# Moving an expert's output bias from VectorE's read of the result into TensorE's accumulation

## The chip, the cores and the metric

The kernel runs on one core of a Trainium2 chip. The metric is device time in microseconds (us), and lower is better. Three runs of the kernel before took 2040.01, 2044.2 and 2039.57 us, with a median of 2040.01 us.

## The reference

The reference is four layers on 4096 tokens of width 128 (16 sequences of 256 tokens). The change touches only layer 0, whose attention part is a selective state scan (256 inner channels, 16 states) and whose feed-forward part is a mixture of 16 experts, of which 12 have weights. For each of those twelve:

```
h = gelu(x_e @ w1[e] + b1[e])      # x_e: up to 512 tokens x 128, h: 512 x 512
y = h @ w2[e] + b2[e]              # 512 x 128
```

The rows y are written to a buffer in memory, from which each token later gathers the two rows that it is owed and adds them with their weights. Everything is float32.

## The kernel before, in words

In `mamba_scan` the state scan and the twelve experts of layer 0 run in one interleaved program. The scan is cut in 128 steps q: one step handles two states of one sequence for both halves of the channels, so it holds two units i = 2q and 2q + 1. For every unit

- ScalarE writes the decays exp(delta * a) in a PSUM bank (L874, two instructions),
- GpSimd multiplies the input with the spread-out B rows (L740),
- VectorE runs the scan (L952) and multiplies its result with the spread-out C rows (L958),
- TensorE adds the product over the states in the bank Y (L785).

Once a step, TensorE spreads C (`spread_c`, L770) and B (`spread_b`, L761) over the partitions, and ScalarE copies B to SBUF (L884). VectorE's product L958 waits for `c_ready`, which the last L770 of its step raises; ScalarE's copy L884 waits for `b_ready`, which L761 raises. Once a sequence there are also the gate product (L965), the skip term (L778), the output projection (L798, L799) and its copy (L888).

Each engine's order is written out by hand. TensorE's order in a step is: `spread_c(q)`, `sum_states(2q-1)`, `spread_b(q+2)`, `expert(q, 0)`, at the first step of a sequence the skip term, `sum_states(2q)`, at one step the projection, `expert(q, 1)`. There is no reordering, so what stands in `expert` stands ahead of the next `spread_c`.

An expert takes a new place every 6 steps. Its work: transpose of its tokens (L836), copy (L896), first product (L828, four matmuls 128x512 in two steps), gelu by ScalarE (L905, four), second product (L811), VectorE's read of the result with the bias (L971) and the store. The second product fills four blocks of 128 tokens of bank 7 (`E1_BANK`), one block in each `expert(q, part)` call of two successive steps; a block is four float32 matmuls 128x128 that accumulate over the hidden width. The first block waits for the last gelu of the expert (`act_done`). The last block raises `y_ready`, and VectorE reads the bank after the first unit of the next step.

The expert's weights lie packed in `ew`; columns B2 to B2 + 128 hold the bias b2, the same row in all 128 partitions. `g.ident` is the 128x128 float32 identity.

Of the kernel before, what the change touches and what calls it, by code (L numbers as in the profile page):

```python
# [9 lines left out]
ALU = mybir.AluOpType  # L10
# [3 lines left out]
P = 128  # L14
D = 128
# [24 lines left out]
FC = F0 // P  # L40
# [38 lines left out]
def rows(ap):  # L79
    return ap.rearrange("p a b -> p (a b)")  # L80
# [515 lines left out]
def mamba_scan(nc, g, t, u, gate_d, delta, bc3, sel, disp, ybuf, r, scattered, f):  # L596
# [4 lines left out]
    DA, C_BANK, E0_BANK, BO, Y_BANK, E1_BANK = 0, 3, 4, 5, 6, 7  # L601
    RING = 3
    NE, CT = E0 - FIRST_MLP0, CAP0 // P
    W2, B1, B2, WN = FC * P, 2 * FC * P, 2 * FC * P + FC, 2 * FC * P + FC + D
# [8 lines left out]
    with section(nc, "scan", *names, "skip_made", "skip_used", "zeroed", "du_ready", "b_ready", "b_copied", "bu_made",  # L613
# [10 lines left out]
        ew = s.sb("ew", [P, 2, WN])  # L624
        exin = s.sb("exin", [P, 2, CT, D])
        ext = s.sb("ext", [P, CAP0])
        eht = s.sb("eht", [P, FC, CAP0])
        eyo = s.sb("eyo", [P, CT, D])
# [7 lines left out]
        def bank(i):  # L636
            return g.ps[:, i, :].rearrange("p (n t) -> p n t", t=T)

        def row(i):
            return sel[:, i:i + 1].to_broadcast([3 * 2 * DS, P])  # L640

        def phase(q, offset):
            e, rest = divmod(q - FIRST - offset, SPACING)
            return e if rest == 0 and 0 <= e < NE else None
# [11 lines left out]
        with nc.Block() as block:  # L656
# [93 lines left out]
            @block.tensor  # L750
            def _(pe):
                def spread_b(q):
                    if q >= NQ:
                        return
                    b, pr = divmod(q, PAIRS)
                    if q >= 1:
                        pe.wait_ge(s.b_copied, q)
                    if b >= 1 and pr == 4:
                        pe.wait_ge(s.o_taken, b)
                    for n in range(2):  # L760
                        ins = nc.tensor.matmul(bank(BO)[:, n, :], row(2 * pr + n), bc3[:, b * T:(b + 1) * T],  # L761
                                               start=True, stop=True)
                    ins.then_inc(s.b_ready, 1)

                def spread_c(q):
                    b, pr = divmod(q, PAIRS)
                    if q >= 1:
                        pe.wait_ge(s.hc_ready, 2 * q)
                    for n in range(2):
                        ins = nc.tensor.matmul(bank(C_BANK)[:, n, :], row(DS + 2 * pr + n),  # L770
                                               bc3[:, b * T:(b + 1) * T], start=True, stop=True)
                    ins.then_inc(s.c_ready, 1)

                def skip_term(b):
                    if b >= 1:
                        pe.wait_ge(s.yg_ready, b)
                    pe.wait_ge(s.skip_made, b + 1)
                    nc.tensor.matmul(g.ps[:, Y_BANK, :], g.ident[:], rows(skip[:]), start=True,  # L778
                                     stop=False).then_inc(s.skip_used, 1)

                def sum_states(i):
                    q, c = divmod(i, DC)
                    pe.wait_ge(s.hc_ready, i + 1)
                    for n in range(2):
                        ins = nc.tensor.matmul(bank(Y_BANK)[:, c, :], g.ident[:], hc[:, i % RING, n, :], start=False,  # L785
                                               stop=(i % (PAIRS * DC) == PAIRS * DC - 1 and n == 1))
                    ins.then_inc(s.sum_done, 1)

                def project(b, ahead):
                    pe.wait_ge(s.yg_ready, b + 1)  # L790
                    if ahead < NQ:
                        pe.wait_ge(s.b_copied, ahead)
                    else:
                        pe.wait_ge(s.combined, 2 * NGRP)
                    for k in range(QT):
                        out = g.ps[:, BO, k * D:(k + 1) * D]
                        for c in range(DC):
                            nc.tensor.matmul(out, yg[:, c, k * P:(k + 1) * P], w_out[:, c, :], start=(c == 0), stop=False)  # L798
                        ins = nc.tensor.matmul(out, g.ident[:], g.x[:, b * QT + k, :], start=False, stop=True)  # L799
                    ins.then_inc(s.o_ready, 1)  # L800

                def expert(q, part):
                    for half, offset in ((0, DOWN0), (1, DOWN1)):
                        e = phase(q, offset)
                        if e is None:
                            continue
                        pe.wait_ge(s.act_done, (e + 1) * FC)
                        i = 2 * half + part
                        out = g.ps[:, E1_BANK, i * D:(i + 1) * D]
                        for f in range(FC):  # L810
                            ins = nc.tensor.matmul(out, eht[:, f, i * P:(i + 1) * P],  # L811
                                                   ew[:, e % 2, W2 + f * P:W2 + (f + 1) * P], start=(f == 0),
                                                   stop=(f == FC - 1))
                        if i == CT - 1:
                            ins.then_inc(s.y_ready, 1)
                    for half, offset in ((0, UP0), (1, UP1)):
                        e = phase(q, offset)
                        if e is None:
                            continue
                        if half == 0 and part == 0:  # L820
                            pe.wait_ge(ew_in[e % 2], (e // 2 + 1) * 16)
                            pe.wait_ge(s.xt_ready, e + 1)
                        if half == 0 and part == 1 and e >= 1:
                            pe.wait_ge(s.y_out, e)
                        if half == 1:
                            pe.wait_ge(s.act_done, e * FC + part + 1)
                        f = 2 * half + part
                        nc.tensor.matmul(g.ps[:, (E0_BANK, E1_BANK)[part], :], ew[:, e % 2, f * P:(f + 1) * P], ext[:],  # L828
                                         start=True, stop=True).then_inc(s.h_ready, 1)
                    e = phase(q, TURN)  # L830
                    if e is not None and part == 1:
                        pe.wait_ge(ex_in[e % 2], (e // 2 + 1) * 16)
                        if e >= 1:
                            pe.wait_ge(s.act_done, e * FC)
                        for i in range(CT):
                            ins = nc.tensor.transpose(g.ps[:, E0_BANK, i * P:(i + 1) * P], exin[:, e % 2, i, :],  # L836
                                                      g.ident[:])
                        ins.then_inc(s.turned, 1)

                spread_b(0)  # L840
                spread_b(1)
                for q in range(NQ):
                    b, pr = divmod(q, PAIRS)
                    spread_c(q)
                    if q >= 1:
                        sum_states(2 * q - 1)
                    if b >= 1 and pr == 3:
                        spread_b(q + 1)
                    elif not (b >= 1 and pr == 2):
                        spread_b(q + 2)  # L850
                    expert(q, 0)
                    if pr == 0:
                        skip_term(b)
                    sum_states(2 * q)
                    if b >= 1 and pr == 2:
                        project(b - 1, q + 2)
                    if b >= 1 and pr == 3:
                        spread_b(q + 2)
                    expert(q, 1)
                sum_states(NU - 1)  # L860
                project(BATCH - 1, NQ)
# [81 lines left out]
            def _(dve):  # L943
                v = nc.vector
# [22 lines left out]
                def take_result(e):  # L967
                    dve.wait_ge(s.y_ready, e + 1)
                    if e >= 1:
                        dve.wait_ge(s.stored, e * 16)  # L970
                    v.tensor_tensor(eyo[:], g.ps[:, E1_BANK, :].rearrange("p (t d) -> p t d", d=D),  # L971
                                    ew[:, e % 2, None, B2:B2 + D].to_broadcast([P, CT, D]), ALU.add).then_inc(s.y_out, 1)

                def combine(j, k):
                    dve.wait_ge(weighted[k], j + 1)
# [7 lines left out]
                for q in range(NQ):  # L983
# [4 lines left out]
                    e = phase(q, DOWN1 + 1)  # L988
# [2002 lines left out]
```

## Time and profile before

| | before |
|---|---|
| median of 3 runs | 2040.01 us (2039.57 to 2044.2) |
| profiled execution: time | 2040.01 us |
| profiled execution: span, first to last instruction | 2038.2 us |
| mean granted TensorE clock (1 is 2.4 GHz) | 0.883 |
| TensorE matmul busy | 1564.5 us (77%) |
| VectorE busy | 1293.2 us (63%) |
| ScalarE busy | 1057.1 us (52%) |
| GpSimd busy | 797.3 us (39%) |
| scan with experts | about 220 to 585 us of the span |
| scan with gather | about 585 to 820 us |

The profiled execution has the median's time, 1.8 us more than its span. In the rows PE is TensorE's matmul, PEld its weight load, DVE VectorE, ACT ScalarE and POOL GpSimd; busy matmuls overlap, since their ends are modelled, so starts are the better measure. A float32 matmul is two records, each with a weight load and a matmul: L811 has 384 records for 12 x 4 x 4 = 192 matmuls. In matmul records the operands are listed as output<-moving,stationary. A row of the timeline gives start, duration, engine, line, operation, count, and in brackets the idle time before it with what ended it.

### The profile page before, as it was taken

Reading aid. Unit: us, or ns where it says so; the run is one execution under the profiler, and the core shown is the slowest. Engines: PE = TensorE matmul, PEld = TensorE weight load, DVE = VectorE, ACT = ScalarE, POOL = GpSimd, SP = SyncE. Lnnn points to the kernel's source line nnn. Section 1 sums busy time; section 2 is a strip of 40 time slices with the busy share of each in tenths; the row PEclk is TensorE's granted clock in tenths of the full one; section 3 lists DMA queues with packets and bytes.
Section 4 is the critical chain, followed back from the end, with each engine's and each line's share of the span. In section 5 each row is a group of like instructions: output and inputs, shape, how many; then the busy total and the mean of one; then the engine's idle time right before and its main releaser. Section 6 shows DMA issues by size and latency. Waiting matters only on the chain. (4 is left out here: it accounts for less than half of the span.)

```text
span 2038.2 us, 34107 instructions
## 1 busy us (share of the span) xinstructions
PE 1564.5 (77%) x12145; PEld 1073.5 (53%) x12146; DVE 1293.2 (63%) x2310; ACT 1057.1 (52%) x1921; POOL 797.3 (39%) x803
## 2 busy tenths in 40 slices
PE   6918688888877667641999999984699999749975
PEld 5605366665654444510667776652245444537853
DVE  7403888787788888751644457858763897624324
ACT  1204888887876666240544455554464777314421
POOL 1570566565679997275012233331500000050041
PEclk9959799999998898675899999997699999669987
DMA  5201111111000010571421125512641341211311
GB/s 153 81 30 37 50 54 50 40 48 45 28 27 26 26 32 11 215 214 39 66 58 58 58 57 84 83 26 81 127 86 52 47 66 19 90 52 39 109 41 55
DMA packets 153335, 130.56 MB, mean 64 GB/s; under 512 B 18929, under 2 KB 137864, under 8 KB 152914
## 3 DMA queue, kind: packets, MB, share of 16 engines
q1 hardware_dynamic: 140554, 104.54, 20.9%
q0 software_dynamic: 12544, 23.82, 4.3%
q8 instruction: 100, 1.64, 0.4%
q14 instruction: 65, 0.53, 0.1%
q10 hardware_dynamic: 72, 0.03, 0.0%
HBM read 77.08 MB, written 52.43 MB: 64 GB/s over the span
## 5 line engine op out<-in xcount | busy, mean ns | idle before, releaser
L740 POOL TENSOR_TENSOR xn_t<-xn_t,scan_du 128x512 f32<-128x512 f32 x256 | 321.2, 1273 | 144.4 <-ACT xn_t L884 97.4
L952 DVE TENSOR_TENSOR_SCAN xn_t<-banks,xn_t 128x512 f32<-128x512 f32 x256 | 311.8, 1218 | 73.3 <-ACT banks L874 44.9
L785 PE MATMUL banks<-scan_hc,ident 128*128 128x256 f32 x1024 | 294.9, 414 | 51.1 <-DVE scan_hc L958 51.1
L2383 ACT ACTIVATE att_pr<-banks 128x768 f32<-128x768 f32 (+1 forms) x256 | 234.4, 917 | 126.1 <-PE banks L2275 75.6
L874 ACT ACTIVATE banks<-delta,scan_exp_centre,a_neg 128x255 f32<-128x255 f32 x512 | 266.1, 561 | 15.7 <-DVE xn_t L952 15.1
L785 PEld LDWEIGHTS banks<-scan_hc,ident 128*128 128x128 f32 x1024 | 192.7, 206 | 111.7 <-DVE scan_hc L958 73.6
L958 DVE TENSOR_TENSOR scan_hc<-xn_t,banks 128x512 f32<-128x512 f32 x256 | 175.9, 687 | 25.8 <-PE banks L770 10.9
L2427 DVE TENSOR_REDUCE att_mb<-banks 128x6 f32<-128x768 f32 x128 | 121.8, 956 | 103.3 <-remote 51.6
L2242 PE MATMUL banks<-att_ks,att_qs 48*128 48x256 bf16 (+1 forms) x1024 | 111.8, 275 | 80.1 <-DVE att_mb L2427 30.4
L1009 POOL DMA_INDIRECT disp<-xn_tok,places x128 | 135.6, 1059 | 73.3 <-issue 38.4
L2431 DVE TENSOR_REDUCE att_mb<-banks 128x4 f32<-128x1024 f32 x128 | 153.8, 1222 | 15.9 <-PE banks L2242 10.6
L2291 PE MATMUL banks<-att_pr,att_vx 128*32 128x256 f32 (+1 forms) x2048 | 154.6, 374 | 8.7 <-ACT att_ot L2388 6.8
L884 ACT COPY xn_t<-banks 128x512 f32<-128x512 f32 x128 | 74.8, 584 | 108.3 <-PE banks L761 86.8
L1394 POOL DMA_DIRECT2D ybuf<-att_yo x72 | 39.0, 542 | 207.8 <-DVE att_yo L1379 204.2
L1210 POOL IOTA gau_rev<- 128x8 f32 x1 | 0.1, 138 | 298.8 <-POOLq L76 298.8
L2267 PE MATMUL banks<-att_qs,att_ks 50*128 50x256 bf16 (+1 forms) x1024 | 108.1, 268 | 8.5 <-DMA att_qs<-att_mt 6.7
L2242 PEld LDWEIGHTS banks<-att_ks,att_qs 48*128 48x128 bf16 x1024 | 48.2, 98 | 102.2 <-issue 39.4
L1295 PE MATMUL banks<-grouped_w,att_xt 128*128 x288 | 99.5, 469 | 0.6 <-DVE att_xt L1361 0.4
L1584 POOL DMA_INDIRECT gau_gb<-ybuf,rows x32 | 32.4, 1014 | 146.0 <-DMA ybuf<-gau_eyo 136.6
L1344 ACT ACTIVATE att_a<-banks 128x352 f32<-128x352 f32 x72 | 33.4, 464 | 99.4 <-PE banks L1295 99.4
L770 PE MATMUL banks<-bc,state_sel 96*128 96x256 bf16 x256 | 53.0, 291 | 34.6 <-DVE scan_hc L958 32.4
L449 PE MATMUL banks<-xn_t,w_taps 128*128 128x255 f32 (+2 forms) x256 | 64.0, 399 | 19.4 <-issue 18.2
(384 smaller groups left out, 3290.4 us busy)
## 6 DMA issues: line engine op xcount, KB each, us to landing
scan_ew<-f_packed SPq DMA_DIRECT2D x12, 578.0 KB, 4.1
q_parts<-att_p_parts SPq DMA_DIRECT2D x16, 384.0 KB, 4.2
k_parts<-att_p_parts SPq DMA_DIRECT2D x16, 384.0 KB, 6.1
att_qs<-q_parts SPq DMA_DIRECT2D x64, 96.0 KB
att_ks<-k_parts SPq DMA_DIRECT2D x64, 96.0 KB
gau_ew<-f_packed SPq DMA_DIRECT2D x8, 578.0 KB
disp<-zeros SPq DMA_DIRECT2D x1, 4608.0 KB, 15.4
att_xin<-disp SPq DMA_DIRECT2D x72, 64.0 KB
```

Source lines behind the costliest of these rows:

```text
L740: nc.gpsimd.tensor_tensor(bu[:, i % RING], b_sb[:, q % 2], du[:, b % 2, c:c + 1, :].to_broadcast([P, 2, T]), ALU.mult).then_inc(s.bu_made, 1)
L785: ins = nc.tensor.matmul(bank(Y_BANK)[:, c, :], g.ident[:], hc[:, i % RING, n, :], start=False, stop=(i % (PAIRS * DC) == PAIRS * DC - 1 a ...
L874: ins = nc.scalar.activation(bank(DA + i % RING)[:, n, 1:T], delta[:, c, b * T + 1:(b + 1) * T], ACT.Exp, scale=a_neg[:, c, state:state + ...
L952: v.tensor_tensor_scan(rows(h[:, i % 2]), g.ps[:, DA + i % RING, :], rows(bu[:, i % RING]), 0.0, ALU.mult, ALU.add).then_inc(s.scan_done, 1)
L958: v.tensor_tensor(hc[:, i % RING], h[:, i % 2], bank(C_BANK), ALU.mult).then_inc(s.hc_ready, 1)
L1009: pool.indirect_dma_start(disp, bass.IndirectOffsetOnAxis(ap=r.scat_i[:, k, i:i + 1], axis=0), src[:, i, :], None, bounds_check=disp.shape ...
L2242: ins = nc.tensor.matmul(g.ps[:, 2 * m_slot(i) + half, lo:hi], qs[rows_of, p, j, q * P:(q + 1) * P], ks[rows_of, p, j, 0:hi - lo], start=T ...
L2267: ins = nc.tensor.matmul(g.ps[:, 2 * s_slot(i) + half, k * T:k * T + T - q0], ks[rows_of, p, j, k * P:(k + 1) * P], qs[rows_of, p, j, q0:T ...
L2291: ins = nc.tensor.matmul(g.ps[r * 32:(r + 1) * 32, O_BANK, q0:T], vx[:, b % 2, k, 4 * jg + r, :], pr[:, i % RING, half, k * T:k * T + T - q0],
L2383: nc.scalar.activation(pr[:, i % RING], g.ps[:, at:at + 2, 0:W], ACT.Exp, scale=scale).then_inc(s.p_ready, 1)
L2427: v.tensor_reduce(mb[:, b % 2, j, :].rearrange("p (g n) -> p g n", g=2), g.ps[:, at:at + 2, 0:W].rearrange("p g (n k) -> p g n k", k=P), A ...
L2431: v.tensor_reduce(mb[:, b % 2, j, :], g.ps[:, at:at + 2, :].rearrange("p g (n k) -> p (g n) k", k=T), AX_X, ALU.max).then_inc(s.m_taken, 1)
```

## The change

Each block of the second product gets a fifth matmul. Its stationary operand is column 0 of the identity, broadcast to 128 columns, so its first row is ones and the others zeros, and its moving operand is the bias row: it adds b2 to each of the 128 tokens. It is the last of the accumulation and takes over `stop` and, in the last block, the increment of `y_ready`. VectorE's read of the bank becomes a plain copy.

```diff
@@ expert(q, part), TensorE @@
                         for f in range(FC):
-                            ins = nc.tensor.matmul(out, eht[:, f, i * P:(i + 1) * P],
-                                                   ew[:, e % 2, W2 + f * P:W2 + (f + 1) * P], start=(f == 0),
-                                                   stop=(f == FC - 1))
+                            nc.tensor.matmul(out, eht[:, f, i * P:(i + 1) * P],
+                                             ew[:, e % 2, W2 + f * P:W2 + (f + 1) * P], start=(f == 0), stop=False)
+                        ins = nc.tensor.matmul(out, g.ident[:, 0:1].to_broadcast([P, P]), ew[:, e % 2, B2:B2 + D],
+                                               start=False, stop=True)
                         if i == CT - 1:
                             ins.then_inc(s.y_ready, 1)
@@ take_result(e), VectorE @@
-                    v.tensor_tensor(eyo[:], g.ps[:, E1_BANK, :].rearrange("p (t d) -> p t d", d=D),
-                                    ew[:, e % 2, None, B2:B2 + D].to_broadcast([P, CT, D]), ALU.add).then_inc(s.y_out, 1)
+                    v.tensor_copy(rows(eyo[:]), g.ps[:, E1_BANK, :]).then_inc(s.y_out, 1)
```

## Rows read from the trace of the kernel before

**Rows 1.** Windows: each engine's busy time (instructions), granted clock, DMA share and GB/s.
```profile
220.00:585.00 365.00, 305.40 (x1586) 225.34 (x1586) 297.13 (x331) 299.10 (x511) 228.77 (x190) 0.96 0.15 45
820.00:2038.00 1218.00, 965.06 (x9387) 642.83 (x9385) 702.44 (x1514) 548.47 (x990) 290.05 (x349) 0.87 0.32 76
```

**Rows 2.** Waits, 220 to 580 us: us in total, times, longest.
```profile
ACT xn_t L884 <- PE banks L761: 47.8, 37, 3.0
PE banks L811 <- ACT scan_eht L905: 18.9, 12, 3.3
DVE scan_hc L958 <- PE banks L770: 10.9, 8, 2.0
```

**Rows 3.** Timeline of one expert's second product, from its first matmul to VectorE's read.
```profile
282.89 1.16 PE L811 MATMUL banks<-scan_ew,scan_eht 128*128 128x128 f32 x8 [1.19 <-ACT scan_eht L905]
283.88 1.03 PE L785 MATMUL banks<-scan_hc,ident 128*128 128x256 f32 x4
...
284.75 1.05 PE L811 MATMUL banks<-scan_ew,scan_eht 128*128 128x128 f32 x8
...
285.64 0.60 PE L836 MATMUL banks<-ident,scan_exin 128*128 128x128 f32 x4
...
286.08 0.38 PE L770 MATMUL banks<-bc,state_sel 96*128 96x256 bf16 x2
...
286.55 0.69 DVE L958 TENSOR_TENSOR scan_hc<-xn_t,banks 128x512 f32<-128x512 f32 x1
...
287.38 1.05 PE L811 MATMUL banks<-scan_ew,scan_eht 128*128 128x128 f32 x8
...
289.14 1.05 PE L811 MATMUL banks<-scan_ew,scan_eht 128*128 128x128 f32 x8
...
290.03 0.38 PE L770 MATMUL banks<-bc,state_sel 96*128 96x256 bf16 x2
...
290.51 0.69 DVE L958 TENSOR_TENSOR scan_hc<-xn_t,banks 128x512 f32<-128x512 f32 x1 [0.28 <-DVE xn_t L952]
...
291.11 0.68 DVE L971 TENSOR_TENSOR scan_eyo<-banks,scan_ew 128x512 f32<-128x512 f32 x1
291.12 0.38 PE L761 MATMUL banks<-bc,state_sel 96*128 96x256 bf16 x2
...
291.54 0.59 ACT L884 COPY xn_t<-banks 128x512 f32<-128x512 f32 x1 [0.93 <-PE banks L761]
291.71 1.22 DVE L952 TENSOR_TENSOR_SCAN xn_t<-banks,xn_t 128x512 f32<-128x512 f32 x1
```

**Rows 4.** Windows of TensorE alone, two experts: busy (records), clock, DMA.
```profile
282.89:290.40 7.51, 7.51 (x55) 1.00 0.12 35
394.92:404.04 9.12, 9.12 (x55) 0.82 0.10 30
```

**Rows 5.** Timeline, VectorE's product before its read, in other experts.
```profile
261.94 0.69 DVE L958 TENSOR_TENSOR scan_hc<-xn_t,banks 128x512 f32<-128x512 f32 x1 [0.33 <-DVE xn_t L952]
345.53 0.69 DVE L958 TENSOR_TENSOR scan_hc<-xn_t,banks 128x512 f32<-128x512 f32 x1 [1.40 <-issue]
576.57 0.69 DVE L958 TENSOR_TENSOR scan_hc<-xn_t,banks 128x512 f32<-128x512 f32 x1 [1.02 <-issue]
```

**Rows 6.** One line's instructions, L2554: duration min/median/max in ns, starts.
```profile
L2554 PEld LDWEIGHTS banks<-norm_mix,mixes_lora_bi x2: 192/192/192, 853.7 to 853.8; 128*128 128x128 f32 x2
L2554 PE MATMUL banks<-norm_mix,mixes_lora_bi x2: 275/275/275, 853.8 to 853.9; 128*128 128x128 f32 x2
```

**Rows 7.** Groups of instructions by shape, VectorE: busy us, mean ns, idle before.
```profile
L971 DVE TENSOR_TENSOR scan_eyo<-banks,scan_ew 128x512 f32<-128x512 f32 x12 | 8.2, 684 | 0.0
L539 DVE COPY front_dtx<-banks 128x512 f32<-128x512 f32 x8 | 5.5, 689 | 28.2 <-PE banks L422 21.1 <-remote 7.0
```

**Rows 8.** Timeline of TensorE, the expert whose second product begins at 394.92 us.
```profile
394.92 2.08 PE L811 MATMUL banks<-scan_ew,scan_eht 128*128 128x128 f32 x8 [1.19 <-ACT scan_eht L905]
...
396.78 1.75 PE L785 MATMUL banks<-scan_hc,ident 128*128 128x256 f32 x4
```

## The prediction

> **What bounds the kernel now.** I read the windows first, to see how full the engines are where the change lies. In the stage that holds scan and experts no engine is full: of 365 us TensorE's matmuls fill 305.4, VectorE 297.1, ScalarE 299.1 [rows 1]. Some 60 us of TensorE's time look free, and on the average alone one would say that 48 short matmuls vanish in them. So the average can't settle it, and I went to the waits of the stage. Three of them tell how the engines hang together: TensorE waits twelve times for ScalarE's gelu before the second product, once an expert (18.9 us); ScalarE waits for the spread B rows of TensorE (37 times, 47.8 us); VectorE's product waits for the spread C rows (10.9 us) [rows 2]. The stage is a ring of four engines that wait for one another in a fixed order, and the question is who is last in the very place where the matmuls are added.
>
> The timeline of one expert answers that. Its second product begins at 282.89, when the gelu is done. From there the reader is to follow TensorE's starts: two blocks of L811 (282.89 and 284.75) with sums and a transpose between them, L770 at 286.08, two more blocks (287.38 and 289.14), L770 at 290.03 [rows 3]. TensorE's window over this stretch is 7.51 us long and busy for 7.51 us [rows 4]: not a gap. At its end L770 starts at 290.03 and takes 0.38, so it ends at 290.41, and VectorE's product starts at 290.51, after 0.28 us of idling [rows 3]. The row names the scan L952 as releaser, but VectorE's own scan is simply the instruction before it; what came 0.10 us before the start is the end of L770, the same distance as between 286.46 and 286.55 one step earlier. ScalarE idles for 0.93 us and starts its copy at 291.54, just after L761 (291.12 + 0.38 = 291.50) [rows 3]. So at the end of an expert's second product VectorE and ScalarE both stand and wait for TensorE, and GpSimd's product needs ScalarE's copy and VectorE's scan. TensorE sets the pace of this stretch from the gelu on, although it doesn't set that of the stage.
>
> I looked at the same place in all twelve experts. VectorE idles ahead of the product that precedes its read in every one: 0.28 us in six of them, 0.33 in three, 1.40 in two and 1.02 in the last [rows 3, 5]. Where "issue" is named, L770 again ended just before. The case of the longer waits is the one where the output projection also stands in TensorE's queue.
>
> **The change part by part.** *Added on TensorE*: a fifth matmul in each block, 12 experts x 4 blocks = 48. Its shape is that of the four before it, 128x128 in float32. Its duration in the rows (about 275 ns a record) isn't what it costs, since matmuls overlap; the distance between starts is. From 284.75 to 285.64, the next instruction's start, four matmuls took 0.89 us, or 0.223 us each (two records of 0.11) [rows 3]. The one thing that is new is the stationary operand, one column repeated. L2554 loads such an operand in float32: its two records start 0.1 us apart and take 192 and 275 ns [rows 6], which is what ordinary ones take, so I take no surcharge. The bounds: below, a single record of 0.11, were the load hidden; above, what a matmul costs at the low clock. That last price is in the trace too: the block at 394.92 took until 396.78, or 0.465 us a matmul [rows 8], at 1.2 GHz (granted 0.82 over the whole stretch, against 1.00 in the other) [rows 4].
>
> The added matmuls of a block stand behind the block and ahead of everything else in TensorE's queue: the sums L785, the skip term, the transpose, the projection, and both spreads. Behind the first two of an expert L770 at 286.08 comes 0.45 us later, and the product at 286.55 starts 0.09 us after its end now: it can't take up a delay of 0.45. Behind all four L770 at 290.03 comes 0.89 later, and the product at 290.51 with it, and L761 and ScalarE's copy too. Every engine had its wait in this stretch already, so none has slack left that would be used up later on; the whole ring moves by 4 x 0.223 = 0.89 us an expert. What comes next, the two L828 of the next expert and its gelu, waits for the same instructions, so it moves as well.
>
> The sum: 48 x 0.223 = 10.7 us. In four of twelve experts (second products from 394.92, 424.60, 511.23 and 540.79; [rows 8] is the first of them) a block or two run at the low clock, so I take 5 of 48 added matmuls at 0.465: + 5 x 0.24 = 1.2 us.
>
> *Removed on VectorE*: the addition of the bias; a copy of the same 128x512 out of PSUM takes its place. L971 takes 684 ns; a float32 copy of 128x512 from PSUM, L539, takes 689 [rows 7]. So that saves nothing: 12 x 0.005 = 0.06 us, if anything as a loss. It would matter if it did save: the read stands between the product and the next scan (290.51, 291.11, 291.71) on the engine that waited. The bounds are nothing and, by the widest guess, a copy in half of L539's time: 12 x 0.34 = 4.1 us. I take nothing, as the copy's row has the same engine, shape, type and memories. The Trainium skill ("VectorE: DVE Perf Modes", "Mode 2×_2P — use both read ports for one tensor") says that a copy in float32 goes twice as fast only with source and target both in SBUF, and that PSUM has one read port; the row of L539 agrees. By its fast mode the sum would be 4.1 us lower, by its rule for PSUM it stays.
>
> *Moved*: `y_ready` is raised by the fifth matmul of the last block, 0.22 us later than before in its block. VectorE asks for it only after the product that waits for L770, which comes still later in TensorE's queue, so this wait is never last. No DMA is added or moved in its queue; SP's store and weight loads wait for the read and shift with it. Nothing in the stages behind the experts changes.
>
> Total: 10.7 + 1.2 + 0.06 = 11.9 us on the profiled execution's 2040.01 us, which is also the median: **2051.9 us**, 0.6% slower.
>
> **The rivals.** *Part of it is hidden.* If the delay of each expert's first two matmuls were taken up, because VectorE's own chain is as late there (it idles only at the second L770, not at the first [rows 3]), only 24 matmuls count: 24 x 0.223 = 5.4, so 2045.4 us. Against it: TensorE is busy without a gap from 282.89 on [rows 4], so what is added at the start is still there at the end. Chance 0.06.
>
> *All is hidden*: the 60 us of TensorE's idle time in the stage [rows 1] take it up. Then 2040.0 us. For that the idle time would have to lie inside the stretch of the second product; it lies before it, in the wait for the gelu [rows 2, 3]. Chance 0.03.
>
> *The clock gives it back, and more.* This is the case that ends faster. After its wait for the gelu TensorE ran at the low clock in the stretch at 394.92, and its 7.51 us became 9.12 [rows 4]. If the added matmuls, by making TensorE busier, kept the clock at 2.4 GHz, each such stretch would get back 1.61 us, four of them 6.4 us, and the result would be 2040.0 + 11.9 - 6.4 = 2045.5. To be faster by 0.3% it must get back 11.9 + 6.1 = 18 us. The stage can't: its clock of 0.96 over 365 us [rows 1] means 2 x 0.04 x 365 = 29 us at half speed, which hold 15 us to gain at most if every one were on the path. It would need the stages behind 820 us, with 0.87 [rows 1], where the kernel is unchanged and only shifted in time. The point from which it decides is thus 36 us of low clock turned to high, half of it on the path. Chance 0.06 for the clock to give back a good part, of which 0.03 for faster. The Trainium skill ("TensorE: Matmul & The Clock Gate", "What's actually happening") says that activity lifts the throttle and idleness sets it; that more matmuls lift it here no row can show.
>
> *Short matmuls are cheaper than the rows' distance.* If a record beside others cost half of what stands between starts now, 0.056 us, the sum would be 48 x 0.11 = 5.3 us and the time 2045.3. The rows speak against it: eight records behind one another take 0.89 us at full clock [rows 3]. Chance 0.02. The Trainium skill ("TensorE: Matmul & The Clock Gate", "Back-to-back issue gap") has a gap of about 56 ns for 128 columns of bf16, the distance of this rival; the trace has 0.11 for a float32 record.
>
> **How the numbers follow.** My forecast, the delay in full, has chance 0.83. Its own range is 10.7 us with no low clock at all to 10.7 + 48 x 0.24 x 0.25 = 13.6 with a quarter of them at low clock, and 1.5 us either side for where the low clock falls in the later stages (the three runs of before spread over 4.6 us): 2049 to 2055. The partly hidden case, the short matmuls and the clock at 2045.4 are taken in as well: the whole range is 2045 to 2055.5. About 0.3%, or 6.1 us, is what a measurement of this kernel tells from no change. Slower by more (over 2046.1): 0.83. Within: 0.06 + 0.03 + 0.03 + 0.02 = 0.14. Faster: 0.03.
>
> **What the profile of the changed kernel would show.** TensorE's records at the second product grow by 96, starts 0.11 us apart. From the gelu to the second L770's end an expert at full clock takes 7.51 + 0.89 = 8.4 us, still without a gap. VectorE's idle time before the product that precedes its read grows by about 0.45 us (0.28 to about 0.7), since the other 0.45 is met at the first L770; there an idle time of about 0.4 appears that is not there now. L971 keeps its 0.68 to 0.69 us. The stage from the first scan to the last expert's read is 11 to 12 us longer, the stages behind it as long as before. I would be wrong if an expert's period of 6 steps grew by less than 0.8 us though its TensorE stretch grew by 0.89 (then there is slack that I missed), if the new load took longer than an ordinary one, or if the clock's low stretches moved by more than a few us.

## The result and the profile after

The changed kernel took 2054.34 us in the median of nine runs (2047.3 to 2057.14), the kernel before 2043.53 us in nine (2039.57 to 2048.34). The ratio is 1.0053, with a 95% interval of 1.0038 to 1.0068: slower by about 11 us, between 8 and 14. The prediction, 2051.9 us with slower at 0.83, holds, and its sum of 11.9 us lies inside that interval. The absolute time came out 2.4 us over it although the difference came out 1.1 us under, since the kernel before itself took 3.5 us more in nine runs than in the three that the prediction started from. The profiled execution took 2063.16 us with a span of 2061.4 us, which is 8.8 us above the median of its runs, so this one profile is read by its stretches and not by its whole span.

The timeline of the changed kernel at the place of [rows 3]; L813 is the added matmul, and the lines behind it are numbered one higher than before:

```profile
281.95 1.16 PE L811 MATMUL banks<-scan_ew,scan_eht 128*128 128x128 f32 x8 [1.12 <-ACT scan_eht L906]
...
282.94 0.39 PE L813 MATMUL banks<-scan_ew,ident 128*128 128x128 f32 x2
283.17 1.03 PE L785 MATMUL banks<-scan_hc,ident 128*128 128x256 f32 x4
...
285.58 0.38 PE L770 MATMUL banks<-bc,state_sel 96*128 96x256 bf16 x2
...
286.06 0.69 DVE L959 TENSOR_TENSOR scan_hc<-xn_t,banks 128x512 f32<-128x512 f32 x1 [0.54 <-PE banks L770]
...
289.76 0.39 PE L813 MATMUL banks<-scan_ew,ident 128*128 128x128 f32 x2
289.99 0.38 PE L770 MATMUL banks<-bc,state_sel 96*128 96x256 bf16 x2
...
290.46 0.69 DVE L959 TENSOR_TENSOR scan_hc<-xn_t,banks 128x512 f32<-128x512 f32 x1 [0.73 <-DVE xn_t L953]
291.07 0.68 DVE L972 COPY scan_eyo<-banks 128x512 f32<-128x512 f32 x1
...
291.49 0.59 ACT L885 COPY xn_t<-banks 128x512 f32<-128x512 f32 x1 [1.40 <-PE banks L761]
```

The added matmul stands from 282.94 to 283.17, 0.23 us. At the first L770 VectorE now idles 0.54 us where its row showed nothing (0.45 us of delay and the 0.09 us that were there); at the second it idles 0.73 us in place of 0.28, and ScalarE 1.40 in place of 0.93. TensorE's stretch, in the windows of the changed kernel (columns as in [rows 1]):

```profile
281.95:290.36 8.41, 8.41 (x63) 7.94 (x64) 5.88 (x7) 7.76 (x14) 4.70 (x5) 1.00 0.10 31
```

Against 7.51 us and 55 records [rows 4] that is 0.90 us and 8 records more, without a gap. The whole stage from the first to the last scan takes 605.0 us (scans start from 221.1 to 826.1) against 592.0 (223.7 to 815.7): 13.0 us more, and all of it lies ahead of the last expert's read (366.4 us from the first scan against 353.4). What lies behind the last scan took 1235.3 us against 1222.5, though nothing is changed there. In the first eight experiments below that part took between 1210 and 1225 us, on either side of before, and 1223.8 with the same added matmuls (e2); I take the 12.8 us for scatter of the single execution.

### The profile page after: what moved, and what is told of

It is laid out like the page before. It is cut to its first block and busy times, and to the rows that moved or that the text cites. A ratio compares the mean times of both kernels' runs of the same rounds, so it can differ in the third digit from the quotient of the medians.

```text
span 2061.4 us, 34299 instructions
## 1 busy us (share of the span) xinstructions
PE 1583.8 (77%) x12241; PEld 1089.1 (53%) x12242; DVE 1293.2 (63%) x2310; ACT 1056.0 (51%) x1921; POOL 796.1 (39%) x803
## 5 line engine op out<-in xcount | busy, mean ns | idle before, releaser
L770 PE MATMUL banks<-bc,state_sel 96*128 96x256 bf16 x256 | 53.3, 292 | 35.2 <-DVE scan_hc L959 32.4
L2267 PEld LDWEIGHTS banks<-att_qs,att_ks 50*128 50x128 bf16 x1024 | 39.9, 95 | 71.7 <-issue 41.4
```

What stands on the lines that cost most here:

```text
L2267: ins = nc.tensor.matmul(g.ps[:, 2 * s_slot(i) + half, k * T:k * T + T - q0], ks[rows_of, p, j, k * P:(k + 1) * P], qs[rows_of, p, j, q0:T ...
```

## The experiments

Ratios are to the kernel before on the same chip, with 95% intervals. Because the whole kernel's runs scatter by some us, I also read from each profile one stretch in which nothing but the scan and the experts runs: from the start of the second expert's second product to the start of the twelfth's, ten experts' periods. It holds ten experts' work, so the change's 48 matmuls count there with 40.

| kernel | ratio (interval) | stretch of ten periods, us | granted clock in it |
|---|---|---|---|
| before | 1 | 285.37 | 0.97 |
| the change | 1.0053 (1.0038 to 1.0068) | 295.78 | 0.96 |
| e1_copy_only | 0.9999 (0.998 to 1.0018) | 285.17 | 0.96 |
| e2_matmul_only | 1.0057 (1.0035 to 1.0079) | 295.92 | 0.96 |
| e3_two_more | 1.0105 (1.0082 to 1.0129) | 304.69 | 0.97 |
| e4_first_half | 1.0001 (0.9979 to 1.0023) | 286.93 | 0.98 |
| e5_last_half | 0.9995 (0.9978 to 1.0013) | 288.75 | 0.97 |
| e6_bf16 | 1.0005 (0.9986 to 1.0024) | 286.18 | 0.98 |
| e7_in_gelu_wait | 0.9965 (0.9946 to 0.9984) | 283.03 | 0.98 |
| e9_act_read_pool_add | 0.9999 (0.9984 to 1.0014) | 289.02 | 0.95 |
| e10_filled_waits | 0.9948 (0.993 to 0.9965) | 277.85 | 1.00 |
| e11_change_filled | 1.0003 (0.9987 to 1.0018) | 286.83 | 1.00 |
| e12_before_again | 1.0009 (0.9993 to 1.0026) | 288.84 | 0.95 |
| e13_gelu_wait_again | 0.9965 (0.9949 to 0.9981) | 280.56 | 0.99 |

The last four ran on a chip on which the kernel before took 1864.04 us (median of 35), since the parts around the scan were shorter there; their ratios are to that.

**The two halves of the change.** First VectorE's half alone:

```diff
-                    v.tensor_tensor(eyo[:], g.ps[:, E1_BANK, :].rearrange("p (t d) -> p t d", d=D),
-                                    ew[:, e % 2, None, B2:B2 + D].to_broadcast([P, CT, D]), ALU.add).then_inc(s.y_out, 1)
+                    v.tensor_copy(rows(eyo[:]), g.ps[:, E1_BANK, :]).then_inc(s.y_out, 1)
```

> VectorE's read is the plain copy, as in the changed kernel, and TensorE has no added matmul; the addition of b2 is left out. My theory: the copy costs what the addition did (L539 took 689 ns, L971 684), so the time stays within 1 us of before and the read stays at 0.68 us. Rival, the copy is the gain that the matmuls buy: at half of 0.68 us it would save 12 x 0.34 = 4.1 us, and the changed kernel's loss would hide that gain.

Measured 2041.27 us against 2042.64. The line of its read in the profile (duration min/median/max in ns, first and last start in us), to set beside [rows 7]:

```profile
L971 DVE COPY scan_eyo<-banks x12: 683/684/686, 260.1 to 574.5; 128x512 f32<-128x512 f32 x12
```

The copy takes the addition's 684 ns to the ns, and the kernel its time. The interval alone, 4 us either way, would just leave room for the rival's 4.1; the row and the stretch of ten periods (285.17 us against 285.37) rule it out. Then TensorE's half alone:

```diff
@@ expert(q, part), in before; the four matmuls of the loop have stop=False @@
+                        ins = nc.tensor.matmul(out, g.ident[:, 0:1].to_broadcast([P, P]), ew[:, e % 2, B2:B2 + D],
+                                               start=False, stop=True)
```

> The 48 added matmuls alone; VectorE keeps its addition, so b2 is added twice. My theory: the whole change in time is TensorE's, so this takes as long as the changed kernel, 11 to 13 us over before (+10.8 us was measured for the change, and the stage from the first scan to the last was 13.0 us longer in its profile). Rival, the two halves of the change balance: this is slower than the changed kernel by as much as the copy saves, 4 us.

Measured 2052.09 us, by the ratio 11.6 us more (7 to 16); its stage from first to last scan is 605.2 us (the change: 605.0) and its stretch 295.92 us (295.78). So the loss is TensorE's alone, and no gain of VectorE's stands behind it.

**More of the same.**

```diff
@@ the changed kernel @@
+                        nc.tensor.matmul(out, g.ident[:, 0:1].to_broadcast([P, P]), ew[:, e % 2, B2:B2 + D],
+                                         start=False, stop=False)
                         ins = nc.tensor.matmul(out, g.ident[:, 0:1].to_broadcast([P, P]), ew[:, e % 2, B2:B2 + D],
                                                start=False, stop=True)
```

> The changed kernel with a sixth matmul in each block, equal to the fifth, so b2 is added twice. My theory: there is no slack anywhere in the second product, so each matmul counts 0.223 us at full clock; 96 of them cost 21.4 us plus 2 to 3 us for those at the low clock, twice the change's own. Expected over before: 22 to 25 us. Rival, the first added matmuls pay for a fixed delay (a longer accumulation, the new kind of stationary operand), and the next are cheaper: under 18 us. Rival, the clock stays up with more work: under 18 us too, with a mean clock over the scan stage nearer to 1.

Measured 2061.51 us against 2042.64, by the ratio 21.4 us more (17 to 26), just under the 22 to 25 that I expected; the stage is 615.8 us, 23.8 over before. The expert that begins at 283.77 runs at full clock:

```profile
283.77:293.07 9.30, 9.30 (x71) 8.83 (x72) 5.80 (x7) 7.77 (x14) 5.58 (x5) 1.00 0.09 28
```

7.51, 8.41 and 9.30 us with none, four and eight added matmuls: each costs 0.22 us, the first as much as the second. So the rival of a fixed delay falls. The rival of a clock that stays up falls by the stage and by the granted clock of 0.97 in the ten periods, the same as in before; the runs' interval, which reaches down to 17 us, would not exclude it by itself.

**Where the matmul stands.** Half of them each, ahead of the first or of the second spread of C (`half` is 0 or 1) in e4 and e5, with VectorE's addition kept:

```diff
@@ expert(q, part), in before; in these blocks the four matmuls of the loop have stop=False @@
+                        if half == 0:        # e4; half == 1 in e5
+                            ins = nc.tensor.matmul(out, g.ident[:, 0:1].to_broadcast([P, P]),
+                                                   ew[:, e % 2, B2:B2 + D], start=False, stop=True)
```

> Before with the added matmul in the first two blocks of each expert only (24 in all), and VectorE's addition kept. My theory: nothing of the delay at the first spread of C is taken up, although VectorE does not idle there before; so half of the full cost, 24 x 0.223 = 5.4 us, and 1 to 2 us more, since it is the first blocks that meet the low clock: 5.4 to 7.5 us over before. Rival, VectorE's chain is as late there and hides it: 0 to 2 us.

> Before with the added matmul in the last two blocks of each expert only (24), and VectorE's addition kept. VectorE idles at least 0.28 us in the product ahead of its read, so these matmuls are on the path without question: 24 x 0.223 = 5.4 us over before, hardly any of it at the low clock: 5 to 6 us. The two halves add up to the whole, 11 to 13 us, if the delay passes on in full everywhere; if the first half is hidden, this one alone makes up the whole.

Both came out within noise of before, where I had expected 5.4 us and more; 5.4 us lies outside both intervals (at most +4.7 and +2.7 us). Yet in both profiles the stretch from the first L811 to the second L770 of an expert, 7.14 us at full clock in before (282.89 to 290.03), was 7.59 and 7.60 us in the second expert: 0.45 us more, as reckoned, for the first half as for the second. It is not made up later in the expert either: an expert's period that ran wholly at full clock took 28.09 or 28.69 us in before, by its place in the sequence, and 28.53 or 28.54 and 29.13 in both of these, 0.44 to 0.45 us more. The stage from the first to the last scan was 594.5 us with the first half and 597.8 with the second, 2.5 and 5.8 over the 592.0 of before. So the profiles hold the delay, and the medians of the twelve runs do not show it. That is a miss of my expectations, and its cause stays open; what the clock can have to do with it is said below.

**Cheaper matmuls.**

```diff
+        none_b = s.sb("none_b", [P, D], BF16)
...
+                nc.gpsimd.memset(none_b[:], 0.0)
...
@@ expert(q, part), in before; the four matmuls of the loop have stop=False @@
+                        ins = nc.tensor.matmul(out, g.ident_b[:, 0:1].to_broadcast([P, P]), none_b[:],
+                                               start=False, stop=True)
```

> Before with a fifth matmul in each block whose operands are bf16, a column of the identity repeated and a tile of zeros; VectorE keeps its addition. My theory: the cost is TensorE's time in the place, whatever it adds. bf16 matmuls of 256 columns (L770 to L785, 0.22 us for two) go 0.11 us apart, so one of 128 columns takes 0.06 to 0.11 us; 48 x that is 2.7 to 5.3 us over before. Rival, a fifth matmul costs by being one more instruction with one more weight load, not by its passes: 10 us or more as in float32.

The same stretch of the second expert took 7.48 us (282.11 to 289.59), 0.34 more than before's 7.14, or 0.085 us a matmul, and the time did not change measurably (48 x 0.085 = 4.1 us is inside the interval, the rival's 10 us are not). The delay goes with the time that the added matmul takes TensorE, not with the number of instructions: a bf16 matmul of this shape is one record and 0.085 us, a float32 one two records and 0.223 us.

**In a wait.**

```diff
@@ expert(q, part), in before @@
+                        if half == 0 and part == 0:
+                            pe.wait_ge(s.act_done, (e + 1) * FC - 1)
+                            for _ in range(2):
+                                nc.tensor.matmul(g.ps[:, E0_BANK, 0:D], g.ident[:, 0:1].to_broadcast([P, P]),
+                                                 ew[:, e % 2, B2:B2 + D], start=True, stop=True)
                         pe.wait_ge(s.act_done, (e + 1) * FC)
```

> Before, with two matmuls of the same kind an expert put into TensorE's wait for the last gelu: they start when the third gelu is done and write the bank that it read, and their result is thrown away. 24 added matmuls, 24 x 0.223 = 5.4 us of work. My theory: what matters is where they stand, and here the last gelu (0.68 us) still runs, so 0.45 us is hidden and the time stays within 1 us of before. Rival, any work on TensorE in this stage costs its time (through the clock, or the queue): 5 to 6 us over before.

Not only was nothing lost: the kernel was faster, 2036.42 us against 2042.64. Its timeline at one expert, where L810 are the added ones:

```profile
365.76 1.26 ACT L910 ACTIVATE scan_eht<-banks,scan_ew 128x512 f32<-128x512 f32 x2
...
366.50 0.71 PE L810 MATMUL banks<-scan_ew,ident 128*128 128x128 f32 x4 [0.60 <-ACT scan_eht L910]
...
367.08 1.16 PE L816 MATMUL banks<-scan_ew,scan_eht 128*128 128x128 f32 x8
```

They begin after the third gelu. The last of their four records starts at 366.93, ahead of the fourth gelu's end at 367.02, and the second product starts at 367.08, 0.06 us behind that end, the same distance as in before (282.83 and 282.89). The expert's period that ends with this wait, at full clock, is 28.69 us with them (338.39 to 367.08) as without (336.79 to 365.48). The same instruction that costs its whole time behind the block costs nothing here. Where the gain of 7.1 us (by the ratio) comes from, this profile says only in part: its stage is 590.3 us, 1.7 under before, with a granted clock of 0.98 in the ten periods against 0.97.

**VectorE's read.** The prediction had said that the read lies on the path. If so, ScalarE and GpSimd could do it in their waits. ScalarE's copy comes one step later than VectorE's read did:

```diff
@@ scalar: new, called behind decay(2 * q) at phase(q, DOWN1 + 2); gone from vector @@
+                    act.wait_ge(s.y_ready, e + 1)
...
+                    nc.scalar.copy(rows(eyo[:]), g.ps[:, E1_BANK, :]).then_inc(s.y_out, 1)
@@ gpsimd: behind the first product of that step; the store waits for y_added @@
+                            pool.wait_ge(s.y_out, e + 1)
+                            nc.gpsimd.tensor_tensor(eyo[:], eyo[:], ew[:, e % 2, None, B2:B2 + D]
+                                                    .to_broadcast([P, CT, D]), ALU.add).then_inc(s.y_added, 1)
```

> Another way to free VectorE: no added matmul; ScalarE copies the bank to SBUF before its copy of the spread B rows, where it idles 0.93 us or more for TensorE, and GpSimd adds b2 in SBUF where it idles 1.49 us for the scan. My theory: VectorE's read (0.60 us from start to start) is on the path, as VectorE starts its next scan right behind it, so this is faster by up to 12 x 0.60 = 7.2 us: 4 to 7 us under before. Rival, ScalarE's copy of the spread rows comes later and with it GpSimd's product, and the scan waits for that: no gain, or slower.

No gain, where I had expected 4 to 7 us: 2043.16 us against 2042.51. The period of the fourth expert, at full clock in both, is 28.68 us where it was 28.69. Its timeline shows why:

```profile
348.92 0.58 ACT L895 COPY xn_t<-banks 128x512 f32<-128x512 f32 x1 [1.83 <-PE banks L766]
349.40 0.59 ACT L907 COPY scan_ext<-banks 128x512 f32<-128x512 f32 x1
...
349.88 1.07 ACT L879 ACTIVATE banks<-delta,scan_exp_centre,a_neg 128x255 f32<-128x255 f32 x2
...
350.98 1.22 DVE L966 TENSOR_TENSOR_SCAN xn_t<-banks,xn_t 128x512 f32<-128x512 f32 x1 [0.55 <-ACT banks L879]
```

and the kernel before at the same place:

```profile
346.56 0.59 ACT L884 COPY xn_t<-banks 128x512 f32<-128x512 f32 x1 [1.83 <-PE banks L761]
...
347.04 0.59 ACT L896 COPY scan_ext<-banks 128x512 f32<-128x512 f32 x1
...
347.52 1.07 ACT L874 ACTIVATE banks<-delta,scan_exp_centre,a_neg 128x255 f32<-128x255 f32 x2
...
348.62 1.22 DVE L952 TENSOR_TENSOR_SCAN xn_t<-banks,xn_t 128x512 f32<-128x512 f32 x1
```

The chain goes from TensorE's spread of B through ScalarE's two copies and the decays to VectorE's second scan. The decays end at 348.59 in before, and the scan starts at 348.62 without an idle time in the row, because the read filled it by chance to the same instant. Without the read VectorE idles 0.55 us for the decays. A row without idle time doesn't prove that its engine was the last.

This chain is that of the fourth, eighth and twelfth expert. In the other nine the first two scans behind the removed read do start 0.60 us earlier, and from the third on 0.42 or 0.20 us are left of it. In six of the nine that rest is gone at the sixth scan, where VectorE waits for the decays that ScalarE makes behind its gelus. This is that scan in the seventh expert, 20.94 us after the start of its second product, first in this kernel and then in the one before:

```profile
448.61 1.22 DVE L966 TENSOR_TENSOR_SCAN xn_t<-banks,xn_t 128x512 f32<-128x512 f32 x1 [1.29 <-ACT banks L879]
```

```profile
445.54 1.23 DVE L952 TENSOR_TENSOR_SCAN xn_t<-banks,xn_t 128x512 f32<-128x512 f32 x1 [0.88 <-ACT banks L874]
```

VectorE only waits 0.41 us longer there. In the first, fifth and ninth expert 0.42 us are still won at that point. Of these three, only the ninth has the same granted clock in both profiles (0.94), and there the next expert's second product does begin 0.41 us earlier (30.06 us after its own against 30.47). That would make 1.3 us for the three, too little for these runs to show. So VectorE's read was not on the path in three experts, in six ScalarE's gelus and decays take the gain back, and in three it seems to be worth 0.4 us each.

**The clock.** In the stretch of ten periods before and the change had a clock of 0.97 and 0.96, and of the 13.0 us that the stage grew by, 10.7 leave over about 2 us for it. To hold it at full speed, matmuls of zeros were put in TensorE's waits for the gelu:

```diff
+                def keep_busy(n):
+                    for _ in range(n):
+                        nc.tensor.matmul(bank(Y_BANK)[:, 0, :], g.ident[:], g.zeros[:, 0:T], start=False, stop=False)
@@ before the first wait of the second product @@
+                        if half == 0 and part == 0:
+                            keep_busy((2, 2, 6, 0)[e % 4])
                         pe.wait_ge(s.act_done, (e + 1) * FC)
@@ before the wait of the first product's second half @@
+                            if part == 0:
+                                keep_busy((1, 5, 0, 0)[e % 4])
                             pe.wait_ge(s.act_done, e * FC + part + 1)
```

> Before, with matmuls of zeros (128x256, added to the open sum in the bank Y, so the result is the same) in TensorE's waits for the gelu: 6 in the wait of 3.25 us, 5 in that of 2.68, 2 in those of 1.18, 1 in that of 0.83, each about 0.43 us. They leave some idle time in each wait, so they delay nothing. My theory: the low clock comes after these waits and costs 7 us between the first and the last second product of before; with the waits filled the clock holds, and the stage from the first to the last scan takes 585 to 587 us in place of 592.0. Rival, the clock falls whatever TensorE does there: 592 us or more. Rival, the added matmuls stand in the way of the sums that follow: slower than 592 us with the clock at 1.

> The changed kernel with the same matmuls of zeros in the waits. My theory: the change costs 4 x 0.223 = 0.89 us an expert at full clock, 10.7 us in all, and the rest of its 13.0 us in the stage is low clock; so with the clock held, the stage is 10.5 to 11 us longer than that of before with filled waits, and shorter than the 605.0 us of the change. Rival, the excess over 10.7 us has another cause than the clock: 13 us longer again.

> The kernel before, unchanged, as one more kernel. It shows how far two sets of runs of one program lie apart: the ratio within 0.2% of 1, and the stage from the first to the last scan within 0.5 us of the 592.0 and 591.8 us that two profiles gave for it. If the stage differs by some us, then differences of 2 us between single profiles say nothing.

> The kernel with 24 matmuls in TensorE's wait for the last gelu once more, since its median was 0.35% under before, which its stage (590.3 against 592.0 us) explains only in part. If the gain is real the ratio is near 0.9965 again and the interval excludes 1; if it was chance, the ratio is 0.999 to 1.001, and the stage 590 to 591 us.

The windows of the ten periods (columns as in [rows 1]) of before with filled waits, the change with filled waits, before, and before once more:

```profile
224.46:502.31 277.85, 248.96 (x1337) 186.61 (x1337) 230.66 (x259) 234.75 (x398) 172.63 (x142) 1.00 0.15 45
```

```profile
224.41:511.24 286.83, 257.88 (x1417) 195.41 (x1417) 230.70 (x259) 235.30 (x398) 172.49 (x142) 1.00 0.14 43
```

```profile
282.89:568.26 285.37, 240.25 (x1260) 179.02 (x1260) 230.73 (x259) 235.34 (x398) 172.64 (x142) 0.97 0.15 43
```

```profile
225.96:514.80 288.84, 244.19 (x1260) 182.22 (x1261) 230.47 (x259) 235.13 (x398) 172.52 (x142) 0.95 0.14 43
```

With the waits filled the clock is at full speed throughout. The filling itself costs nothing: the periods that before ran wholly at full clock took 28.09, 25.81 and 28.69 us, and those of the filled kernel take 28.08, 25.80 and 28.69. The change then costs 286.83 - 277.85 = 8.98 us in ten periods, 0.898 an expert, 10.8 us for twelve. From the first to the last scan it is 595.3 against 584.3 us, 11.0; the runs, 1863.35 against 1855.28 us, say 8 us, give or take some 4. So of the 13.0 us in the first pair of profiles, what exceeds 10.8 to 11.0 is gone once the clock is held, and no rival cause is needed for it.

The kernel with filled waits has the lowest median of the last four, 1855.28 us against 1864.04 (its stage, 584.3 us, came out just under the 585 to 587 expected), and the one with 24 matmuls in the wait (e13, the same kernel as e7) repeated its 0.9965 to the digit, this time with a stage of 587.6 us and a clock of 0.99. The change with filled waits is level with the plain kernel before. And the second profile of the unchanged kernel missed my expectation for it: its stage took 596.6 us, 4.6 more than 592.0, with a lower clock (0.95 against 0.97). So two single profiles of one program can differ by that much in this stage.

This puts the two half experiments in their place. At full clock their ten periods should take 277.85 + 20 x 0.223 = 282.3 us; they took 286.93 and 288.75, so the low clock cost 4.6 and 6.4 us. In before it cost 285.37 - 277.85 = 7.5 us and in its second profile 11.0. The low clock takes less from them in these profiles than from before, by 1 to 6 us according to which profiles are set side by side. Beside the first profile of before it is 2.9 us for the first half and 1.1 for the second, which is less than the 5.4 us that were missing. So the clock can be part of the answer, and that it is the whole is not shown: these are single profiles, from different chips, and the missing 5.4 us are of medians. Whether the low clock falls more seldom with half of the matmuls than with none or all (9.0 us in the change) was not tried.

## Why the prediction was right, point by point

- **TensorE sets the pace of the second product**: shown. The stretch stays without a gap and grows by what is added, at 0, 4 and 8 matmuls; VectorE's and ScalarE's idle times at its end grow by 0.45 and 0.47 us.
- **48 x 0.223 = 10.7 us**: shown, 10.8 us by the two kernels at full clock. The broadcast column as stationary operand has no surcharge. The rival that a short matmul costs 0.11 us falls.
- **The delay passes on in full**: shown at full clock, 0.898 us an expert. The sign of being wrong, a period that grows by less than 0.8 us, did not come. All and part hidden fall as mechanisms, by the periods at full clock; that 24 of them alone were not measurable in the medians is unexplained, as said.
- **1.2 us for low clock**: the weak term of the sum, not for its price but for its kind. I counted which added matmuls run slowly, five, and in the changed kernel's profile five blocks did have records 0.21 to 0.24 us apart instead of 0.11. What varies is the low clock's cost over all ten periods: 7.5 and 11.0 us for the same program, 9.0 with the change. In the profiled pair the stage grew by 13.0 us in place of the 11 to 12 that I had said; in the medians the change cost 10.8 us, between 8 and 14, which leaves both 0 and 1.2 us for the clock possible. So far as this term is concerned, that the sum of 11.9 came within 1.1 us of the medians' difference is luck.
- **The copy saves nothing**: shown, 684 ns for either, 0.9999 for the kernel.
- **The read "would matter if it did save"**: wrong. Off VectorE it gains nothing measurable: in three experts the spread of B, ScalarE's copies and the decays end at the same time, in six the gain is lost again in front of the decays behind the gelus, and in three about 0.4 us each may be left, not 0.60 in all twelve.
- **The clock rival**: it did not come; the added matmuls behind the blocks left the clock at 0.96 against 0.97. What it said of a gain to be had was right: ten periods hold 7.5 to 11 us to be got back (I had put 15 at most for the stage), and it takes matmuls in the waits to get them. The Trainium skill ("TensorE: Matmul & The Clock Gate", "Why this matters for your kernels") advises to keep TensorE busy and to avoid idle gaps between bursts of matmuls; the row with a clock of 1.00 against 0.97 agrees.
- **The stages behind as long as before**: the one pair of profiles says 12.8 us more, the next eight between 1210 and 1225 us on both sides of 1222.5. I take it for scatter of single executions; no run shows a cause.

## What to carry to other kernels

An engine that is busy 84% of a stage can be the one on which everything waits at one place in it. Look at the place where the work is added, and whether the other engines idle for this one there; the same 0.22 us matmul cost its full time behind the block and nothing in the wait just ahead of it. Moving a fused addition off a read saves nothing if a plain read takes as long; here that left the other engine's time as a pure loss. Before trusting a row without idle time as proof that an engine is last, see what else ends at that moment; and before comparing two single profiles at 0.2%, see the granted clock of the stretch.

## What the runs showed of the hardware that was not expected

- Useless matmuls in the waits made the kernel faster: 0.9948 (0.993 to 0.9965), with the granted clock of ten periods at 1.00 in place of 0.97 and 0.95. The matmuls, of 0.43 us each, stood in waits of 0.83 to 3.25 us.
- A copy of 128x512 float32 from PSUM and the same read with an addition of an SBUF operand both take 684 ns on VectorE.
- The same unchanged program took 2042 to 2044 us on the chips of the first runs and 1864 us on the last. The profiles place the difference outside the scan, whose stage is 592.0 and 596.6 us: the start of the first scan is at 223.7 us on one and at 165.7 on the other. What makes it was not looked into.
